# Layer two's radial features as three bfloat16 parts, its list of long tiles in SBUF, loads issued earlier, one joined row table

## The reference, cut to what matters

```python
h = jnp.maximum(_layernorm(x, axis=-1), 0.0)
x = x + _L0_gnn_ref(h, edge_attr_4, edge_attr_8, ..., edge_index)
h = jnp.maximum(_layernorm(x, axis=-1), 0.0)
x = x + _L1_gnn_ref(h, node_vec1, src, dst, edge_attr_4, edge_attr_10, ...)
# inside layer two (_L1_gnn_ref):
w = relu(edge_length_embedded @ W_fc1 / sqrt(10)) * sqrt(2) @ W_fc2 / sqrt(100)   # 10 -> 100 -> 192
l0, l1 = (x0 @ W_l1_0, x1 @ W_l1_1) * a      # linear map of every node, then gathered by edge_src
si     = (x0 @ W_si0, x1 @ W_si1) * a        # skip part of every node
messages = products of w, l[edge_src] and edge_attr ; s = segment_sum(messages, edge_dst)
out = si + 0.5 * (s @ W_l2) * a / sqrt(96)
```

## Time and profile before

| | |
|---|---|
| median of 3 runs | 2805.22 us (2803.18 to 2820.76) |
| profiled execution: its time | 2816.24 us |
| its span | 2814.5 us |
| mean granted TensorE clock | 0.955 |
| PE busy | 2534.1 us (90%) |
| DVE, ACT busy | 2223.6 and 2223.7 us (79% each) |
| POOL busy | 1932.9 us (69%) |
| DMA | 334.90 MB, mean 119 GB/s |

### The profile page before, as it was taken

One profiled execution on the slowest core, in us unless ns is written; L12 is line 12 of the kernel. 1 busy time (PEld: TensorE's weight loads), 2 busy tenths in 40 slices (PEclk: granted clock), 3 DMA queues, 4 the chain that ended last, 5 costly groups with the idle time before them and its releaser, 6 DMA issues. The chain is left out here.

```text
span 2814.5 us, 95761 instructions
## 1 busy us (share of the span) xinstructions
PE 2534.1 (90%) x27324; PEld 2403.3 (85%) x27324; DVE 2223.6 (79%) x9897; ACT 2223.7 (79%) x6527; POOL 1932.9 (69%) x2035
## 2 busy tenths in 40 slices
PE   2999999999999999999999956888999999899996
PEld 1998898999889999998899956888988888889896
DVE  6999899999999999999999933667666766666664
ACT  3899898988889989988999944667777777677774
POOL 4888888888888888888888813545454454454441
PEclk9999999999999999999999966999998999889997
DMA  4444444444444444444444413555555555555552
GB/s 135 102 116 116 109 118 115 115 116 116 116 116 116 113 122 116 116 115 115 117 117 116 111 53 76 142 130 143 135 138 128 141 145 138 124 135 132 133 134 69
DMA packets 616739, 334.90 MB, mean 119 GB/s; under 512 B 222729, under 2 KB 599801, under 8 KB 616217
## 3 DMA queue, kind: packets, MB, share of 16 engines
q1 hardware_dynamic: 514549, 212.97, 29.9%
q0 software_dynamic: 48736, 83.76, 12.8%
q10 hardware_dynamic: 52932, 32.04, 4.1%
HBM read 197.84 MB, written 130.67 MB: 117 GB/s over the span
## 5 line engine op out<-in xcount | busy, mean ns | idle before, releaser
L724 POOL DMA_INDIRECT xg<-sources,win x501 | 512.4, 1023 | 592.9 <-DMA ee_sb<-in_ee 321.1
L724 POOL DMA_INDIRECT xg<-in_x,win x501 | 770.0, 1537 | 174.1 <-issue 149.5
L1234 PE MATMUL out_ps<-w_out,aggT 128*100 128x64 f32 (+2 forms) x6012 | 641.5, 258 | 4.4 <-ACT aggT L1061 2.3
L1220 PE MATMUL agg_ps<-sel,msg 128*128 128x100 f32 x4512 | 599.4, 284 | 40.1 <-issue 33.2
L1234 PEld LDWEIGHTS out_ps<-w_out,aggT 128*100 128x100 f32 x6012 | 614.4, 173 | 7.0 <-issue 4.3
L1220 PEld LDWEIGHTS agg_ps<-sel,msg 128*128 128x128 f32 x4512 | 552.3, 197 | 52.6 <-issue 44.2
L1050 ACT ACTIVATE msg<-pw,win 128x64 f32<-128x64 f32 x1503 | 417.4, 353 | 3.6 <-DVE pw L869 1.6
L912 DVE SCALAR_TENSOR_TENSOR xo<-out_ps,a_sb,xo 100x160 f32<-100x160 f32 x500 | 169.0, 380 | 219.7 <-remote 101.6
L1098 ACT ACTIVATE ev<-hT_ps,a_sb 100x320 f32<-100x320 f32 x500 | 236.2, 523 | 127.3 <-PE hT_ps L1264 124.3
L1061 ACT COPY aggT<-agg_ps 128x600 f32<-128x600 f32 x377 | 247.8, 657 | 100.6 <-PE agg_ps L1220 33.6
L736 POOL TENSOR_TENSOR rs<-ve,neghalf 128x4 f32<-128x4 f32 x251 | 260.9, 1040 | 20.9
(11 more groups left out here) (155 smaller groups left out, 5808.3 us busy)
## 6 DMA issues: line engine op xcount, KB each, us to landing
sources<-ev SPq DMA_DIRECT2D x500, 125.0 KB
xn<-in_x SPq DMA_DIRECT2D x250, 125.0 KB
xmid<-xo SPq DMA_DIRECT2D x250, 125.0 KB
ev<-xmid SPq DMA_DIRECT2D x250, 125.0 KB
ev<-sources SPq DMA_DIRECT2D x250, 125.0 KB
out<-xo ACTq DMA_DIRECT2D x250, 125.0 KB
win<-in_edge_rec SPq DMA_DIRECT2D x1002, 3.0 KB
ee_sb<-ee_parts SPq DMA_DIRECT2D x501, 18.0 KB
```

The source lines that it names most:

```text
L724: pool.indirect_dma_start(out=xg[:, t.slot, j, 0:D], out_offset=None, in_=edge_rows, in_offset=bass.IndirectOffsetOnAxis(ap=win[:, t.slot, ...
L1220: ins = pe.matmul(sums_ps[t.half][:, j, k * NT:(k + 1) * NT], flat[:, t.half, j, k * P:(k + 1) * P], sel[:, t.half, j, :], start=not t.ser ...
L1234: ins = pe.matmul(rows[0:NT, j, c0:c1], aggT[:, t.half, j, k, :], w[f"out{k}_"][:, :], start=fresh, stop=True, skip_group_check=not fresh)
```

## The change

- **Radial part of layer two.** It becomes what layer one's is: 30 rows (three bfloat16 parts of ten features) in `ee_parts[1]`, loaded three times over to 90 partitions, and two bfloat16 products of 90 rows with the stacked parts of the weight (`fc1_parts1`). `SecondFeatures` makes the table during the first turns of layer one: five chunks of two features, one load each, 15 casts on ACT (two features each), 10 subtractions on DVE, 15 stores and 9 copies of weight parts on SP.
- **List of long tiles.** SP copies it at turn 80 of layer one from DRAM into an unused partition of `ev`. Every engine reads the length at step 120 of each layer's loop instead of at its end, and the fields from SBUF.
- **Loads moved.** At the end of layer one SP issues the `win` and `ee_sb` loads of layer two's first three turns before the long tiles, not after the barrier. SP's wait for all stores moves from ahead of the long tile's loads to behind them (`finish`). The stores of layer one's last six turns are issued by ACT. Layer two's store of the new rows moves from ACT, T(6), to SP, T(7).
- **Joined table.** `middle` [N, 2, D] holds the rows after layer one and the skip part side by side; layer two loads both in one DMA of 200 packets of 1280 bytes in place of two with 200 of 640.
- In the set-up DVE also makes the parts of the second weight (five small instructions), ACT fills half as much of `ee_sb`, and all rows of `long_tab` get defaults.

```diff
@@ run_steps
+        if s == COUNT_AT:            # 3 * LIST_AT = 120
+            n_long = count()
+    return n_long
@@ build
-    xmid = nc.dram_tensor("xmid", [N, D], F32, kind="Internal").ap()
-    sources = nc.dram_tensor("sources", [2, N, D], F32, kind="Internal").ap()
+    middle = nc.dram_tensor("middle", [N, 2, D], F32, kind="Internal").ap()
+    sources = nc.dram_tensor("sources", [N, D], F32, kind="Internal").ap()
@@ class SecondFeatures (new)
+    def sync(self, sp, step):
+        if 0 <= step < self.n:
+            c = step
+            sp.wait_ge(self.s_ee, 16 * (c + 1))
+            if c >= STAGES:
+                sp.wait_ge(self.s_cast, self.casts(c - STAGES, PARTS - 1))
+            sp.dma_start(self.e[:, c % STAGES, :, :], self.ee[self.rows(c), :]...).then_inc(self.s_ee, 16)
+        if 0 <= step - STAGES < self.n:
+            c = step - STAGES
+            sp.wait_ge(self.s_cast, self.casts(c, PARTS - 1))
+            sp.wait_ge(self.s_parts, self.parts0 + 16 * PARTS * c)
+            for g in range(PARTS):
...
+                sp.dma_start(to, self.part[:, c % STAGES, g, :, :]).then_inc(self.s_parts, 16)
+        if step == STAGES + self.n:
...
+    def scalar(self, act, step):
+        for g in range(PARTS):
+            c = step - 1 - g
+            if 0 <= c < self.n:
...
+                    act.wait_ge(self.s_rest, self.rests(c, g - 1))
+                act.copy(self.part[:, c % STAGES, g, :, :], self.e[:, c % STAGES, :, :]).then_inc(self.s_cast, 1)
+    def vector(self, dve, step):
+        for g in range(PARTS - 1):
+            c = step - 1 - g
+            if 0 <= c < self.n:
+                dve.wait_ge(self.s_cast, self.casts(c, g))
...
+                dve.tensor_tensor(e, e, self.part[:, c % STAGES, g, :, :], ALU.subtract).then_inc(self.s_rest, 1)
@@ class LongTiles
+    def copy_list(self, sp):
+        sp.wait_ge(self.s_list, 32)
+        sp.wait_ge(self.s_scat, 16 * TC)
+        sp.dma_start(self.table[:, 0:4 * LISTED], ...).then_inc(self.s_table, 16)
...
+    def count(self, eng):
+        eng.wait_ge(self.s_table, 32)
+        return eng.value_load(self.table[:, 4 * LISTED:4 * LISTED + 1], min_val=1, max_val=TILES)
@@ one_layer: SP's step
-                    sp.dma_start(ev[0:NT, t.slot, :, 0, :], rows_of(node_rows, t)).then_inc(xn_in[t.slot], 16)
-                    sp.dma_start(ev[0:NT, t.slot, :, 1, :], rows_of(sources[1], t)).then_inc(xn_in[t.slot], 16)
-                if (t := T(PRE + 1)) and first:
-                    sp.wait_ge(ev_ready, t.m * PAIR + PAIR)
+                    both = node_rows[bass.ds(t.n * (PAIR * NT), PAIR * NT), :, :].rearrange("(j p) k c -> p j k c", p=NT)
+                    sp.dma_start(ev[0:NT, t.slot, :, :, :], both).then_inc(xn_in[t.slot], 16)
+                if (t := T(PRE + 1)) and first and t.n < NB - LAST:     # LAST = 6
+                    store_rows(sp, t)
+                if (t := T(7)) and not first:
+                    sp.wait_ge(rows_ready, t.m + 1)
                     sp.dma_start(rows_of(new_dram, t), xo[0:NT, t.slot, :, 0:D]).then_inc(stored[t.slot], 16)
+                if first and T(0):
+                    second_features.sync(sp, T(0).n)
@@ one_layer: SP behind the loop
-            for k in range(RING):
-                sp.wait_ge(stored[k], per_store * len(range(k, NB, RING)))     # now in finish()
+            if first:
+                sp.load(regs, starts[0:1, 0:RING * PAIR])
+                sp.wait_ge(sel_ready, NB)
+                sp.wait_ge(she_ready, NB)
+                sp.wait_ge(hid_done, NB)
+                second_features.stored(sp)
+                for n in range(AHEAD):
+                    for j in range(PAIR):
...
@@ one_layer: ACT's step
+                if (t := T(0)) and first:
+                    second_features.scalar(act, t.n)
...
-                if (t := T(6)) and not first:
-                    store(t)
+                if (t := T(PRE)) and first and t.n >= NB - LAST:
+                    store_rows(act, t)
@@ one_layer: DVE's step, last
+                if (t := T(0)) and first:
+                    second_features.vector(dve, t.n)
@@ one_layer: PE, radial
-                        ins = pe.matmul(hid_ps[0:fc1.shape[1], j, :], fc1[:, :], ee_all[0:krad, t.slot, j, :], start=True, stop=True)
+                        ins = pe.matmul(hid_ps[0:fc1.shape[1], j, :], fc1[:, :], ee_sb[0:krad, t.slot, j, :], start=True, stop=True)
```

More of the change, by code:

```diff
@@ L64 @@
 LIST_AT = 40
+FEATS = 2
+STAGES = 4
+COUNT_AT = 3 * LIST_AT
+LAST = 6
 class Turn:
@@ L212, in build @@
         long_tiles = LongTiles(nc, sb, sem, dict(locals()))
-        for layer, (node_rows, edge_rows, new_dram) in enumerate([(x, x, xmid), (xmid, sources[0], out)]):
+        second_features = SecondFeatures(nc, sb, sem, dict(locals()))
+        win_sems = [[sem(f"win_in{k}_{layer}") for k in range(S1)] for layer in range(2)]
+        for layer, (node_rows, edge_rows, new_dram) in enumerate([(x, x, middle[:, 0, :]), (middle, sources, out)]):
             one_layer(nc, ctx, layer, node_rows, edge_rows, new_dram, dict(locals()))
@@ L522, in one_layer @@
     deep = 1 if first else 2
-    edge_rec, long_tab, long_num, ee = v["edge_rec"], v["long_tab"], v["long_num"], v["ee_parts"] if layer == 0 else v["ee"][1]
+    edge_rec, long_tab, long_num, ee = v["edge_rec"], v["long_tab"], v["long_num"], v["ee_parts"][layer]
     nrow = ee.shape[0]
-    krad = PARTS * nrow + PARTS if first else SW
-    ee_all = ee_sb[:, :, :, 0:P] if first else ee_sb[:, :, :, :].bitcast(F32)
-    fc1 = v["fc1_parts"] if first else w["fc1_"]
+    krad = PARTS * nrow + PARTS if first else PARTS * nrow
+    fc1 = v["fc1_parts" if first else "fc1_parts1"]
+    second_features = v["second_features"]
     hidden = 64 if first else 100
@@ L539, in sem_first @@
         return sem(name) if first else None
-    win_in = [sem(f"win_in{k}_") for k in range(S1)]
+    win_in = v["win_sems"][layer]
     xn_in = [sem(f"xn_in{k}_") for k in range(S1)]
@@ L628, in second_pass, with store_rows @@
             finish(Turn(done + (NB - 1), f + NB, done - 1, RING, 0, 1, True), record, f)
+    def store_rows(eng, t):
+        eng.wait_ge(ev_ready, t.m * PAIR + PAIR)
+        eng.dma_start(rows_of(new_dram, t), xo[0:NT, t.slot, :, 0:D]).then_inc(stored[t.slot], 16)
+        for k in range(2):
+            eng.dma_start(rows_of(made[k], t), ev[0:NT, t.slot, :, k, :]).then_inc(stored[t.slot], 16)
     with nc.Block() as block:
@@ L635, in load_tile @@
                 sp.dma_start(win[:, t.slot, j, :], edge_rec[bass.ds(start, P), :]).then_inc(win_in[t.slot], 16)
[L636 to L639, removed]
+                rows = ee[:, bass.ds(start, P)].unsqueeze(0).to_broadcast([PARTS, nrow, P])
+                sp.dma_start(ee_sb[0:PARTS * nrow, t.slot, j, :], rows).then_inc(win_in[t.slot], 16)
             cols = new_dram.shape[1]
@@ L656, in step @@
                     long_tiles.sync(sp)
+                if (u := T(LIST_AT)) and first and u.n == LIST_AT:
+                    long_tiles.copy_list(sp)
                 if t:
@@ L706, in finish @@
             def finish(t, record, f):
+                for k in range(RING):
+                    sp.wait_ge(stored[k], per_store * len(range(k, NB, RING)))
                 sp.wait_ge(ev_ready if first else rows_ready, t.m * PAIR + PAIR if first else t.m + 1)
@@ L1071, in gates @@
                                ACT.Silu).then_inc(gates_ready, 1)
-            def store(t):
-                act.wait_ge(rows_ready, t.m + 1)
-                act.dma_start(rows_of(new_dram, t), xo[0:NT, t.slot, :, 0:D]).then_inc(stored[t.slot], 16)
             def node_h2(t):
```

141 lines of the change are left out of this document (91 added, 50 removed).

## The result

The changed kernel takes 2922.06 us (median of 4 executions) against 2812.5 us for the kernel before, measured beside it: ratio 1.0372, interval 1.0325 to 1.0419. It is slower by 3.7%. The forecast was 2789 us, with 2890 as its upper end.

A forecast was written before the change was run, and what follows sets the result against it. PE bounded undisturbed layer-two turns, and SP's issues would after the change. 2816.2 + 1.2 + 7 - 19.7 - 6.5 + 2.5 - 0.8 = 2799.9, less 11.0 to the median: 2789 us, range 2715 to 2890.

The forecast's parts named there:

- Theory A: Layer two: SP's issues set the turn at 4.1 to 4.5 us; 2789 us, range 2740 to 2838; chance 0.50.
- Rival B: Layer two: SP is not the limit; 2700 us with today's losses, 2620 with half of them gone; chance 0.15.
- C: Layer two: a slower turn set by the busiest DMA engines; half of it gives 2890 us; chance 0.30.
- The size of SP's turn: Layer two: issues, store, waits and register reload sum to 4.19 us; 4.1 to 4.5 given, 4.3 taken.
- The reload: SP in layer two: reloading sixteen registers every eighth turn costs 1.49 us extra, 0.19 a turn.
- The stalls: Layer two: they and the half clock take 0.71 us a turn now; engines waiting on SP have time to spare.
- The 30 rows in place of 24: Layer two's ee_sb issues on SP: in proportion 0.38 us more a turn, perhaps nothing.
- the tail behind the loads of turn 249: End of layer two: 18.5 us from turn 249's loads to the last rows, an estimate.
- The fill: Layer one's first turns: subtractions on DVE and casts on ACT cost +7 us, between +2 and +14; set-up +1.2.
- The seams: Layer ends: -19.7 us after layer one, -6.5 after layer two; reading the length at step 120, +2.5 for both.
- Rival D: End of layer one: the early loads bring nothing and the long tile still starts late; 2808 us; chance 0.05.
- PE's gain: Layer two: bfloat16 products cut PE's turn by 0.31 us to 3.18, but the saving stands idle behind SP.

The follow-up runs named there:

- e2: Changed kernel with layer two's 90 radial rows loaded feature by feature, the three copies side by side; 2999.05 us, ratio 1.068 to the kernel before.
- e7: Changed kernel with layer two's table standing three times over in memory, so a load is a plain block of 90 rows; ratio 1.0201 to the kernel before.
- e1: Changed kernel with the store of layer two's new rows back on ACT; 2858.01 us, ratio 1.0176 to the kernel before.
- e6: The e1 kernel with the making of the second table spread over 45 turns; ratio 1.0434 to the kernel before.
- e9: Changed kernel without further edits, run again on chip 12, where the long stalls are absent; ratio 1.1005 to the kernel before.
- e12: Changed kernel with the table stored three times over from SBUF, row store on ACT, table making spread over 81 turns; 2460.96 us, ratio 0.9699 to the kernel before.
- e10: The kernel before, unchanged, run for its trace on chip 12; ratio 1.0007.
- e4: Changed kernel without the radial part: layer two's stays float32, no second table; 2752.63 us, ratio 0.9808 to the kernel before.

## Why the prediction was wrong

*What bounds layer two: right.* Theory A named SP's issues, 4.1 to 4.5 us a turn, above PE's 3.18. The waits after, e2 (issues of 0.92 to 0.96 us, a turn of 5.01, same bytes) and e7 (issues of 0.34 to 0.35 us, SP's turn of 3.19) show it. Rival B, that SP is no limit, is out. C, with its 0.30 and the range's upper end of 2890 us, stood for a slower turn that the busiest DMA engines set. No run shows single engines, so no run shows the term behind that end. What the runs showed in its place: in e1 and e6 every transfer has the same form and bytes, and the turn falls by what SP no longer issues (from 4.67 to 4.44 us, in the second condition from 4.51 to 4.01); `ee_sb`'s issue did not grow beyond 0.76 to 0.83 us, and the mean DMA share of the changed kernel stayed at 0.55. C was right in sign, since the kernel is slower, but it is SP's issues that the runs point to. In B two numbers don't follow from the rows: the losses are 0.71 us and not 0.76, and with half of 0.76 gone the time is 2789 - (4.30 - 3.56) x 246 = 2607 us and not 2620.

*The size of SP's turn: the step that failed.* The sum was 4.19 us, given as 4.1 to 4.5, taken as 4.3, for the 246 turns between the first issue and the loads of turn 249. Measured over just these, (2879.64 - 1720.33)/246, are 4.71. (Over all 249 turns, from the first `ev` load to the last, (2885.49 - 1723.32)/249, they are 4.67, since the last three have no tile loads.) The 0.52 us between 4.19 and 4.71 are four terms:

- A normal turn was summed as 3.53 + 0.37 + 0.1 = 4.00 us; where nothing disturbs it, it is 4.19 to 4.20: +0.19. The store is 0.38 + 0.05, and from its end to the next load are 2107.22 - 2106.74 = 0.48 us, which I put down to waits and arithmetic, where the fill's gap was 0.23 and I had allowed 0.1 more.
- The reload costs 2.1 us every eighth turn, 0.26 a turn, not 0.19: +0.07. With it the turn is 4.45, inside the bounds.
- Some turns are longer even in the second condition, where the same 246 turns take 4.55 (e9): +0.10, not taken apart.
- The stalls were put at nothing, because an engine held up by SP would have that much to spare. From 4.55 to 4.71 they take 0.16 us a turn: +0.16. The argument was right in direction, for the kernel before lost 0.71, and e1 with its shorter SP turn loses 4.44 - 4.01 = 0.43. It was wrong in taking the rest for nothing: with SP at its limit 0.16 us a turn was not made up.

The 30 rows in place of 24 cost nothing: an issue takes 0.76 to 0.77 us with either. Against the 4.30 that was taken, 0.41 x 246 is 101 us, and the tail behind the loads of turn 249 took 21.1 us in place of 18.5: together the 104 by which layer two missed its forecast of -0.8.

*The fill: missed outside its bounds.* +8.2 with the set-up, up to 14 for the fill; measured +23.8. The work of DVE and ACT was counted, its dependence on SP was not. The nine weight copies appeared in the change's own list and in no term: 6.97 us in front of a turn's loads. ACT's wait for the first features was no term either, though the diff puts the wait ahead of ACT's whole turn. Of the 27.5 us of e9, e6 takes away 14 by placing alone.

*The seams: right.* End of layer one -17.7 with -19.7 forecast; end of layer two -6.8 with -6.5; length read at step 120 +2.3 in layer one with +2.5 for both, and 0.8 in the second condition. Rival D is out: the early loads do let the long tile start behind the last turns. Layer two's head start was counted as none beyond the three turns, and the first issue indeed stayed 6.8 us behind the long tile's `ev`. That layer two's end could have given more was overlooked: with the store on ACT the span behind the last new rows is 12.3 us (e1), with it on SP 20.6.

*PE's gain: 0.31 us a turn forecast, 0.26 found.* Taken for dead behind SP, it was; e12 shows it once SP's turn lies below PE's. The stalls' 0.71 us a turn, which the forecast carried as a property of the kernel, is one of the condition: e10 has none. The half clock that the forecast saw behind the stalls is in the trace of the kernel before: PE stood for 2.24 us ahead of its product at 2053.96, then its granted clock was 0.61 over 2054 to 2056 us and 0.50 over 2056 to 2060 us, and twelve products (L1220) took 2.85 us in place of 1.48.

The sum of the misses in the spans: fill 15.6, layer two 104.1, seams and reads 3.4, together 123 us. Another 10 come from the step from the profiled execution to the median: 11.0 us were taken off, as in the kernel before, and the changed kernel's profiled execution lay only 1.2 above its median. That makes the 133 us between 2789 and 2922, against a range that reached 101 us above its centre.

## What to carry to other kernels

Count the queue that issues the transfers as an engine: sum its issues, waits, gaps between issues and register reloads for a turn, and hold the sum against the engine that bounds the turn before making that engine faster. Where it comes out above, take the sum near its upper bound and add part of the stalls (here 0.16 us a turn, where the kernel before lost 0.71). Take the gaps between issues from a steady turn; from the last issue of a turn to the next turn's first load the fill had 0.23 us, the steady turn 0.48. Work that was "hidden in the fill" had three prices here: its own time on engines already full and the place of its waits in each engine's order (of 27.5 us, 13.4 stayed when the work was spread, e6), and every small DMA that it put ahead of a load (nine in 6.97 us).

## What the runs showed of the hardware

- The length of an issue on SP depended on the form of the source: 90 rows of 256 bytes took 0.34 us as a plain block, 0.76 us as a block repeated three times, 0.92 to 0.96 us with each row repeated three times. Layer one's 72 rows and layer two's 90, both a block repeated three times, take 0.76 to 0.77 us. The issue behind it differed too: the joined load of 200 packets of 1280 bytes took 0.46 us behind a block repeated three times (e9), 0.33 us behind a plain block (e7, e12) and 0.50 us where each row was repeated (e2, the median of 250).
- The same kernel took 2811 us in one set of runs and 2538 to 2539 in others, on different chips (11; 9 and 12). In the latter, PE in layer one is busy 999.8 of 1000 us (in the former 96%), and the kernel before shows no stall of up to 4 us. Whether the chip is the cause or something else that differed between the sets was not tested.
- With SP near its limit the turn lost less to these stalls, but not nothing: 0.71 us a turn in the kernel before and about 0.6 in e4, where SP has slack, 0.43 in e1, 0.16 in the changed kernel.
